# A fused attention and expert kernel: setup rebuilt, part of an expansion on ScalarE, and a new order of the first expert slots

## The reference

```python
x = x + xattn(layernorm(x), ctx, ctx, Wq, bq, Wk, bk, Wv, bv, Wd, bd)
x = x + ffn(layernorm(x), w_red, wg, W1, b1, W2, b2)

def xattn(q, k, v, ...):          # 16 heads of 16
    query = (q @ Wq.T + bq).reshape(B, -1, H, D)     # key_p, value likewise
    logits = einsum('bsid,bsjd->bsij', query, key_p) / sqrt(D)
    out = einsum('bsij,bsjd->bsid', softmax(logits), value)
    return transpose(out, (0, 2, 1, 3)).reshape(B, -1, O) @ Wd.T + bd

def ffn(hidden, ...):             # 8 experts, one for each token
    wg_n = wg / maximum(norm(wg, axis=1), 1e-4)
    gates = softmax((x @ w_red) @ wg_n.T)
    scores, idx = max(gates), argmax(gates)
    h = gelu(x @ W1[idx] + b1[idx]);  o = h @ W2[idx] + b2[idx]
    return o * scores
```

## Time and profile before

| | |
|---|---|
| time, median of 3 runs | 436.13 us (432.74 to 436.34) |
| the profiled execution | 435.58 us, span 433.7 us |
| PE busy | 384.0 us, 89% |
| DVE busy | 312.9 us, 72% |
| POOL busy | 297.8 us, 69% |
| ACT busy | 234.6 us, 54% |

### The profile page before, as it was taken

How to read it: one execution, slowest core, us unless ns; L and a number is a source line. 1 busy time by engine, 2 the same in 40 slices (tenths; PEclk the granted TensorE clock), 3 DMA queues, 4 the chain that set the end, 5 groups by cost and what they waited for, 6 DMA issues and landing times.

```text
span 433.7 us, 11372 instructions
## 1 busy us (share of the span) xinstructions
PE 384.0 (89%) x3785; PEld 306.2 (71%) x3785; DVE 312.9 (72%) x667; ACT 234.6 (54%) x781; POOL 297.8 (69%) x399
## 2 busy tenths in 40 slices
PE   3998799999999889899797587988999999999990
PEld 3776577666767667656565475777999999999970
DVE  0564899988989889999999774578465555556640
ACT  2334378868768587777562465563244444444420
POOL 1568668869779587786765965565377777777751
PEclk9699899999999999999999898999899999999996
DMA  5776668697796788966575500131012222222200
GB/s 168 228 201 200 159 186 225 204 243 197 211 242 193 203 210 229 249 187 166 160 169 164 149 27 26 50 115 50 26 63 76 74 69 66 68 66 68 66 18 0
DMA packets 97513, 59.31 MB, mean 137 GB/s; under 512 B 70446, under 2 KB 88527, under 8 KB 97456
## 3 DMA queue, kind: packets, MB, share of 16 engines
q1 hardware_dynamic: 92336, 48.44, 40.9%
q0 software_dynamic: 3744, 9.53, 7.5%
q10 hardware_dynamic: 1376, 0.61, 0.5%
HBM read 37.41 MB, written 22.07 MB: 137 GB/s over the span
## 4 chain that ended last, share of the span: by engine, by line
PE 46%; DVE 16%; DMA 14%; issue 10%; POOL 7%; SPq 3%; ACT 2%; DVEq 1%; ACTq 0%; POOLq 0%
PE bQ L1079 14%; DMA qkv_scr<-qkv 10%; PE bKV L1047 8%; PE bL L1047 6%; PE bKV L897 4%; POOL kx L368 4%; DMA ql<-qkv_scr 2%; PE bL L905 2%; DVE qkv L472 2%; PE bO L905 2%; PE bY L933 2%; PE bQ L969 2%; DMA wgT<-in_L_ffn_wg 2%; SPq L244 2%; PE bT L1061 2%
## 5 line engine op out<-in xcount | busy, mean ns | idle before, releaser
L368 POOL TENSOR_TENSOR kx<-ql,mask 128x2048 f32<-128x2048 f32 x32 | 117.9, 3683 | 40.0 <-issue 28.3
L1079 PE MATMUL bQ<-w,wA 128*128 x312 | 74.3, 381 | 3.3 <-DVE r L712 2.7
L462 DVE TENSOR_TENSOR ax<-bA,mask 128x2048 f32<-128x2048 f32 x32 | 73.3, 2290 | 0.6 <-PE bA L985 0.6
L1079 PEld LDWEIGHTS bQ<-w,wA 128*128 128x128 f32 x312 | 56.2, 190 | 10.6 <-issue 4.5
L897 PE MATMUL bKV<-wA,xcT 128*128 128x512 f32 x128 | 61.9, 607 | 1.4 <-DVE qkv L472 1.4
L391 POOL DMA_INDIRECT out<-r,isc x39 | 41.3, 1059 | 22.3 <-issue 13.4
L349 POOL TENSOR_TENSOR rs<-ve,half 128x2 f32<-128x2 f32 x39 | 28.3, 726 | 24.9 <-ACT ve L733 24.8
L414 POOL DMA_INDIRECT r<-row_scr,ig x39 | 40.5, 1038 | 6.0 <-issue 2.4
L842 ACT ACTIVATE wA<-bL,r 128x128 f32<-128x128 f32 x76 | 21.6, 367 | 41.3 <-PE bL L1047 26.6
L842 ACT ACTIVATE wA<-bKV,r 128x128 f32<-128x128 f32 x80 | 22.8, 368 | 37.6 <-PE bKV L1047 20.8
L905 PE MATMUL bO<-ax,pad 128*32 128x128 f32 x1024 | 36.2, 284 | 6.7 <-DVE ax L462 6.4
(11 more groups left out here) (200 smaller groups left out, 726.9 us busy)
## 6 DMA issues: line engine op xcount, KB each, us to landing
qkv_scr<-qkv SPq DMA_DIRECT2D x32, 384.0 KB, 3.5
ql<-qkv_scr SPq DMA_DIRECT2D x32, 384.0 KB, 4.4
row_scr<-cat SPq DMA_DIRECT2D x32, 133.5 KB, 3.5
w<-in_L_ffn_W SPq DMA_DIRECT2D x16, 256.0 KB, 4.5
xt<-in_x SPq DMA_DIRECT2D x15, 256.0 KB, 4.8
ct<-in_ctx SPq DMA_DIRECT2D x15, 256.0 KB, 5.4
w1b<-in_L_ffn_W SPq DMA_DIRECT2D x12, 256.0 KB, 4.3
w1b<-in_L_ffn_W SPq DMA_DIRECT2D x2, 512.0 KB, 7.8
```

Of the source, the lines that this page charges most:

```text
L368: eng.tensor_tensor(block(kx[:, z % 2, :]), spread_heads(ql[z % 2][:, :, 0:HD]), mask_b, ALU.mult).then_inc(S["kx"], 1)
L462: eng.tensor_tensor(block(ax[:, :]), spread_heads(bA[:, 0:C].rearrange("p (l i) -> p l i", l=NH)), mask_b, ALU.mult).then_inc(S["ax"], 1)
L1079: i_ = eng.matmul(bQ[:, 0:C], hT[b % 2][:, k, :], w2[:, bass.ds(eb * (KH * C) + k * C, C)], start=(k == 0), stop=(k == KH - 1))
```

## The change

Setup: wgT is no longer loaded but made from wgb with the identity as a mask. Tiles 0 and 1 of x and ctx are loaded apart. TensorE's order and VectorE's order are new, and two of the four weight copies are ScalarE's. The two casts of the iotas move to the start. Wd, bd and b1 are loaded behind tile 2; the two whole weights of experts 0 and 1 (EARLY_IN) become halves, two at t = 0 and two at t = 1. POOL's constants move from t = 1 to t = 0. For t < 4 ScalarE turns a tile before it takes the moments of the next.

Steps 24 to 30: VectorE writes blocks 3 to 7 of `ax`, then ScalarE blocks 0 to 2.

Slots: `vector_up` is cut in two, the copy of W1 (`vector_up`) and gT (`vector_turned`). `tensor_rows` and `vector_turned` move into the next step, behind the products of bL and behind the softmax's subtraction; `vector_down` goes before `vector_up`. The first gather moves into step 32, ahead of kx, and the second into slot 1. ScalarE's row operations stand behind the exponential from t = 32.

```diff
-EARLY_IN = 2
-HALVES_IN = 1
+HALVES_IN = 0
+DOUBLE = (0, 1)
...
+                if t == FIRST + 1:
+                    pool_gather(eng, 0)
...
-                if t == 1:
+                if t == 0:
                     pool_constants(eng)
...
-            for a in (0, 1) if s == 0 else (s + 1,):
+            for a in () if s == 0 else (1, 2) if s == 1 else (s + 1,):
...
         def vector_setup(eng):
-            weight_copy(eng, 0, 1)
-            eng.wait_ge(S["ld_g"], 48)
+            eng.wait_ge(S["iotas"], 1)
+            for wide, row, n in ((io_r, io_r1, P), (io_k, io_k1, NSP)):
+                eng.tensor_copy(wide[:, :, :], row[:, :].unsqueeze(2).broadcast_to((P, n, NT // 2))
+                                ).then_inc(S["wide"], 1)
+            eng.wait_ge(S["wtr"], 1)
+            eng.tensor_copy(*weight_place(1)).then_inc(S["wTk"], 1)
+            eng.wait_ge(S["ld_w0"], 16)
...
+            eng.wait_ge(S["ld_g"], 32)
...
+            eng.tensor_tensor(wgd.rearrange("p (e g) -> p e g", e=NE), wgb[0:NG].rearrange("p (e g) -> p e g", e=NE),
+                              ident[0:NG, 0:NG].unsqueeze(1).broadcast_to((NG, NE, NG)), ALU.mult).then_inc(S["wgd"], 1)
+            eng.wait_ge(S["wgd"], 1)
+            eng.tensor_reduce(wgT[:, :], wgd.rearrange("p (e g) -> p e g", e=NE), AX, ALU.add)
...
+            b = SHARE if shared(s1) else 0
+            eng.tensor_tensor(block(ax[:, :])[:, :, b:, :],
...
+        def scalar_expand(eng, s1):
+            eng.wait_ge(S["ax0"], s1 + 5 - ROUTE)
+            for b in range(SHARE):
+                i_ = eng.activation(block(ax[:, :])[:, :, b, :], bA[:, 0:C].rearrange("p (l i) -> p l i", l=NH), ACT.Copy,
+                                    scale=mask[:, b:b + 1])
+            i_.then_inc(S["ax"], 1)
...
+                for s in SLOTS_AT.get(t, ()):
+                    vector_turned(eng, s - 2)
...
                 for s in SLOTS_AT.get(t, ()):
+                    vector_down(eng, s)
                     vector_up(eng, s)
-                    vector_down(eng, s)
+            vector_turned(eng, LAST - FIRST - 1)
...
                     blocks(eng, bL, pad[:, s0 % 3, 0:2 * C], kx[:, s0 % 2, :]).then_inc(S["qk"], 1)
+                slots = SLOTS_AT.get(t, ())
+                for s in slots:
+                    tensor_rows(eng, s - 1)
...
-                for s in slots:
-                    tensor_rows(eng, s)
```

More of the change, by code:

```diff
@@ L32 @@
 LAGSB = 4
+SHARE = 3
 NH2 = NT // 2
@@ L60, with halves_at @@
         "gat0 gat1 gat2 gat3 gat4 gat5 xg sca0 sca1 sca2 sca3 w1s gT rsc up gtr gel down").split()
+def halves_at(t):
+    first = t - HALVES_IN + sum(HALVES_IN <= d < t for d in DOUBLE)
+    return range(first, first + 1 + (t in DOUBLE)) if HALVES_IN <= t < B2_IN else ()
 def live(t):
@@ L267, in sync_attention @@
                                   ).then_inc(S[f"ld_c{n // 2 % 3}"], 16)
-                if t == -1:
-                    for m in range(EARLY_IN):
-                        expert(eng, m, 0, KC)
+                if t == -3:
+                    sync_setup_output(eng)
                 if live(a):
@@ L277, in sync_attention @@
                                   ).then_inc(S[f"ld_q{a % 2}"], 16)
-                m = t - HALVES_IN
-                if 0 <= m < B2_IN - HALVES_IN:
-                    expert(eng, EARLY_IN + m // 2, m % 2, m % 2 + 1)
+                for h in halves_at(t):
+                    expert(eng, h // 2, h % 2, h % 2 + 1)
                 m = t - B2_IN
@@ L456, in vector_setup, with shared @@
                               ALU.add).then_inc(S["mask"], 1)
+        def shared(s1):
+            return ROUTE <= s1 + 4 < ROUTE + 7
         def expand(eng, s1):
@@ L541, in vector_attention @@
                                       .broadcast_to((P, KC, NH, NB)), ALU.mult).then_inc(S["norm"], 1)
-                if t == 1:
-                    eng.wait_ge(S["iotas"], 1)
-                    for wide, row, n in ((io_r, io_r1, P), (io_k, io_k1, NSP)):
-                        eng.tensor_copy(wide[:, :, :], row[:, :].unsqueeze(2).broadcast_to((P, n, NT // 2))
-                                        ).then_inc(S["wide"], 1)
                 if t == ROUTE + 7:
@@ L745, in scalar_ahead @@
             n = t + 2
+            if live(t + 1) and t < 4:
+                scalar_turned(eng, t + 1)
             if live(n):
@@ L758, in scalar_attention @@
                           .broadcast_to((P, NE * NG))).then_inc(S["ld_g"], 16)
-            with nc.allow_non_contiguous_dma("wg transposed and bd by columns, 384 elements"):
-                eng.dma_start(wgT[:, :], wg.rearrange("e g -> g e")).then_inc(S["ld_g"], 16)
+            with nc.allow_non_contiguous_dma("bd by columns, 256 elements"):
+                eng.dma_start(ct[:, 1, :], ctx_in[1]).then_inc(S["ld_c0"], 16)
+                eng.dma_start(xt[:, 1, 0:C], x[1]).then_inc(S["ld_x0"], 16)
                 eng.dma_start(bdc[:, :], bd.rearrange("(a p) -> p a", p=P)).then_inc(S["ld_bc"], 16)
@@ L797, in scalar_attention @@
                     eng.activation(pr, bL[:, 0:C], ACT.Exp, scale=HD ** -0.5).then_inc(S["exp"], 1)
+                if live(d) and t >= NT:
+                    scalar_row(eng, t, d)
                 if t == NT + 2:
@@ L805, in scalar_attention @@
                     moments(eng, w, 1, cat[w % CR][:, 0:C])
+                if live(s1) and shared(s1):
+                    scalar_expand(eng, s1)
                 if t >= 5:
@@ L823, in scalar_attention, with scalar_row @@
                 eng.wait_ge(S["score"], d + 1)
+        def scalar_expand(eng, s1):
[4 more added lines that the diff above has]
+            i_.then_inc(S["ax"], 1)
+        def scalar_row(eng, t, d):
+            eng.wait_ge(S["rs"], t + 2)
+            r = rs[t % 3][:, 1:2]
+            eng.wait_ge(S["nm1"], d + 1)
+            eng.activation(cat[d % CR][:, NB_:NB_ + 1], nm[:, 1:2], ACT.Copy, scale=r).then_inc(S["nb"], 1)
+            eng.wait_ge(S["gsub"], d + 1)
+            if d < HOLD:
+                eng.activation(ge[:, :], glog[:, d, :], ACT.Exp, scale=r,
+                               accum_out=cat[d % CR][:, SC:SC + 1]).then_inc(S["score"], 1)
+            else:
+                eng.activation(gsc[:, d - HOLD, :], glog[:, d, :], ACT.Copy, scale=r).then_inc(S["scaled"], 1)
         def scalar_rows(eng, s):
@@ L863, in tensor_setup @@
             weight_transposes(eng, 1)
+            tensor_turned(eng, 0)
+            fill(eng, 4)
+            weight_transposes(eng, 2)
+            fill(eng, 6)
+            weight_transposes(eng, 0)
             eng.wait_ge(S["pad0"], 1)
-            eng.wait_ge(S["ld_g"], 48)
+            eng.wait_ge(S["ld_g"], 32)
             for k in range(KC):
@@ L893, in tensor_kv @@
             else:
-                eng.wait_ge(S["wT"], 2)
+                eng.wait_ge(S["wTk"], 1)
+                eng.wait_ge(S["wTv"], 1)
             eng.wait_ge(S["xT"], a + 1)
@@ L949, in tensor_attention @@
                     blocks(eng, bO, pad[:, s1 % 3, 2 * C:4 * C], ax[:, :]).then_inc(S["pvo"], 1)
-                slots = SLOTS_AT.get(t, ())
                 for s in slots:
```

91 lines of the change are left out of this document (47 added, 44 removed).

## The result

The changed kernel takes 434.1 us in the median of 18 runs (429.9 to 438.4), the kernel before 436.2 in 18 runs beside it (432.7 to 438.1). Two of the 18 (436.3 and 438.4) were slow executions, and the ratios in this document leave such executions out. The ratio is **0.9946, with a 95% interval of 0.9922 to 0.9969**: 2.4 us faster (1.3 to 3.4) where I said 10.8. The prediction was wrong: 434.1 lies above its range, and my other case of "within 1%", with a chance of 0.05, is what happened.

What follows compares the result with a forecast made beforehand. Bounds: loads and VectorE's order in setup, TensorE from tile 5, VectorE in the routing steps, then a ring of waits. -8.2 - 5.0 + 2.4 = -10.8 us from 435.58 gives 424.8, stated as 425; range 418.5 to 430.5.

Steps and rivals of the forecast that it cites:

- Part 1: Setup: earlier bQ of tile 0 (-6.8 us) and moved casts (-1.4) give -8.2 us, from -1.5 to -9.
- So nothing is lost there: SP's queue after setup: kx of tiles 2 and 3 still ready in time, so no cost from the weight halves.
- rival 5: Steps 5 to 23: reloads decide, SP falls behind, 19 steps at 7.5 us, +16.8, 441.8 us; chance 0.02.
- The term for the casts: Setup: two casts moved to the front cost nothing there and no longer hold VectorE up before bKV; -1.4 us.
- Part 2: Routing steps 24 to 30: expansion shared with ScalarE, -5.0 us, bounds -5.9 and +3.5.
- seven times 0.71: Routing steps 24 to 30: each saves 0.84 us on VectorE less 0.13 lost in waits, together -5.0 us.
- Part 3: Slots where attention ends: earlier gather and kx against vector_down before vector_up, net +2.4 us, bounds -3 and +7.
- 1.4 us more each, and 0.3 at slot 8: Slots at t = 36, 37, 38 and slot 8: cost of gT behind w1's copy behind down, 4.5 us in all.
- Rival 1: Slots at the end: the new order pays as a whole, -3 us there, 419.5 us in total; chance 0.15.
- Rival 4: Routing steps: ScalarE's share gives nothing, rs and oT come 1.24 us later, 430 us; chance 0.05.
- Rival 3: Setup: halves, bias rows or tile 1 land late, setup gains only 3.5 us, 429.5 us; chance 0.10.
- Rival 2: Last slots: the clock falls after the longer stands, three slots lose about 1.5 us each, 429.5 us; chance 0.12.

Runs made afterwards that it cites:

- bias_later: both_moves with the three broadcast bias rows issued behind tile 2, in front of Wd; 0.9649 of the kernel before.
- both_moves: Changed kernel with weight halves issued in front of the wait for the store's landing and vector_up before vector_down; 0.9696 of the kernel before.
- before_halves_first: The kernel before, with each weight half issued in front of the wait for the store's landing, not behind the reload; 0.9888 of the kernel before.
- no_share: Changed kernel with VectorE doing all 8 blocks of the expansion in the seven routing steps; 0.9977 of the kernel before.
- setup_only: Changed kernel with only the rebuilt setup: VectorE does the whole expansion, slots at the end in their old order; 0.9894 of the kernel before.
- up_first: Changed kernel with vector_up called before vector_down in steps t = 31 to 38; 0.9752 of the kernel before.

## Why the prediction was wrong

**Part 1, setup, -8.2 predicted; 6.7 in the trace at tile 5, 4.6 (2 to 7.2) measured alone.** Two steps of it failed. The first is "The two loads left on ld_g land by 2.28 + 6.9 = 9.2 us": that took a landing time from a queue in which the loads stood in another order. It was 8.8 us here and not 6.9, and by bias_later and the kernels with the same edit the bias rows account for most of it. In both_moves, where it was 7.5, the lead at tile 4 is 8.1 us (39.06 - 30.99), near the forecast; here it is 6.8. The second is "So nothing is lost there", on SP: I followed SP through tiles 2 and 3 only. TensorE comes to tile 5 with 6.7 us more in hand, while kx of tile 0 comes 4.3 us sooner (24.11 against 28.45 in the earlier trace rows); the reserve of SP shrank, and in 19 steps 3.3 us were given back. This is **rival 5**, to which I gave 0.02, in a milder form. Its condition ("once the time from q to kx exceeds what two steps leave") was put at the wrong resource; what decides is the round of SP itself, landing plus all issues, against 6.24 us. My argument against it, that "SP has the same work per step as before", was true and beside the point: SP had been near the bound before. In the steady steps of the trace before it is 4.28 us on average from the issue of the store to the issue of the reload (19 steps), which takes 0.54, and a half's issue takes 1.44: 6.3 us, and TensorE's undisturbed step is 6.24. before_halves_first bears it out with its 4.9 us.

"TensorE has no gap over 1 us in front of it" was wrong too (2.73); that bKV ran at full clock is right for this execution and not for all. The term for the casts was right: they cost 1.23 and 0.48 us in their new place, where the second had taken 3.96 beside kx.

```profile
2.10 1.23 DVE L440 CAST io_r<-io_r 128x2048 bf16<-128x2048 f32 x1 [2.10 <-POOL io_k L312]
3.24 0.48 DVE L440 CAST io_k<-io_k 128x640 bf16<-128x640 f32 x1
```

**Part 2, sharing, -5.0 predicted; 1.6 in the trace, 1.4 and 0.5 measured.** This is one of the two largest errors. Each duration was right: ax of 1.49 on VectorE, 1.19 for ScalarE's three, and bO right behind.

```profile
197.65 1.49 DVE L482 TENSOR_TENSOR ax<-bA,mask 128x1280 f32<-128x1280 f32 x1
199.33 1.19 ACT L857 ACTIVATE ax<-bA,mask 128x256 f32<-128x256 f32 x3
200.57 1.08 PE L960 MATMUL bO<-ax,pad 128*32 128x128 f32 x32 [0.24 <-ACT ax L857]
```

The failed step is "seven times 0.71". I had read the bound in the window of the last five steps and gave its saving to all seven; t = 24 and 25 gave nothing and took 16.34 us together where they had taken 15.26 (15.20 in no_share). In step 25 the path through the counts is longer with ScalarE in it. In step 24 it is another thing, which I had not priced: kx started 0.94 us behind bKV, and a VectorE instruction that began beside it took 2.02 us (see the last section). In the ten traces where kx started ahead of bKV there and this instruction took 0.3 to 0.7 us, the step is 6.6 to 6.9 us long, with the sharing or without. In the other five the saving was 0.4 to 0.5 us a step instead of 0.71. Both comparisons exclude 5 us: with their intervals combined they end at 3.5 and 3.2.

**Part 3, slots, +2.4 predicted; +3.6 measured (0.9977 of no_share against 0.9894 of setup_only, with the intervals combined 0.4 to 6.8), and +3.7 in the trace: 6 us from the first up product to the eighth against a lead of 2.3 before it.** The mechanism was the one that I named, gT behind the copy of w1 behind down. From the end of down to the next up it is 2.54, 2.54, 2.90 and 2.53 us at t = 36, 37, 38 and slot 8, where I had 2.5. What was too small is the price of that chain over the old order, "1.4 us more each, and 0.3 at slot 8", less "0.5 for what overlaps". Three up products of the kernel before, to be set beside those above:

```profile
267.40 2.56 PE L1047 MATMUL bKV<-wA,r 128*128 128x128 f32 x16
272.64 1.95 PE L1047 MATMUL bL<-wA,r 128*128 128x128 f32 x16
282.20 1.97 PE L1047 MATMUL bL<-wA,r 128*128 128x128 f32 x16
```

With those at 277.51 and 287.89, the intervals from the third up product to the seventh grew by 1.65, 1.41, 1.96 and 0.59 us: 5.6 where the term had 4.5, and no overlap took any of it back. The lead at the third was 1.7 us over tile 31, and I had 1.6. The first half of the term was right: kx of tile 30 starts 7.5 us sooner (233.32 against 240.83 in the earlier trace rows), 2.5 more than the lead of 5.0 at tile 31, and the first up product keeps 2.3 of it.

The parts measured singly sum to -4.6 - 1.4 + 3.6 = -2.4, the measured whole. That is so by construction, since they are differences of the same ratios; only the single numbers carry information.

**Rivals.** Rival 1 (the order pays) came true only with the one exchange that my own text pointed to: up_first. Rival 4 (the sharing gives nothing) had 0.05 and is nearly what happened. Rival 3 (loads hold the setup) was right in kind. Each rival was weighed alone; that three of them would each come a part of the way was not among my cases, and so the range was too narrow. Rival 2 did not come: no fall followed the gaps of 2.3 us (2.02 us for the 16 products, the usual). The fall behind the stand of 2.86 us at t = 35 (granted clock 0.50 in the 1.9 us behind it) was there before.

## What to carry to other kernels

An engine that only issues DMAs has a round, too: add up its issues and the landing that it waits for, per step, and set that against the pace of the engine that you speed up. If the two are close, a lead won ahead of it will not survive whole, and an issue that nobody waits for belongs in front of the wait, not behind it. When a saving is multiplied by a number of steps, look at the bound of every one of these steps. And when an order of two calls is priced as a loss in the prediction, measure the other order first.
